# Embedding of images 2 to 7 as a two-tap filter with three products for two tokens

## The reference

```python
xp = jnp.pad(x, ((0, 0), (0, 0), (0, PAD), (0, 0)), mode='edge')   # 8 steps at the end
idx = jnp.arange(N)[:, None] * STRIDE + jnp.arange(PATCH_LEN)[None, :]   # patches of 16, stride 8: N = 16
patches = jnp.transpose(xp[:, :, idx, :], (0, 4, 2, 3, 1))
xf = jnp.fft.rfft(patches, axis=-2, norm='ortho')
x_emb = jnp.concatenate([real of xf, imag of xf], axis=-1) @ W.T   # 64 numbers per token
h = jnp.concatenate([cls_tok, x_emb], axis=1)      # 1 + 64*16 tokens per image
h = h + attention(layernorm(h))                    # causal, softmax, D = 64
h = h + experts(layernorm(h))                      # softmax gate over 8 experts, three layers each
```

## Time and profile before

| | us |
|---|---|
| median of 3 runs | 389.95 |
| the three runs | 384.7, 390.22, 389.95 |
| the profiled execution | 389.21 |
| its span, from the first to the last instruction | 387.5 |

### The profile page before, as it was taken

One profiled execution on the slowest core, in us unless ns is written; L12 is line 12 of the kernel. 1 busy time (PEld: TensorE's weight loads), 2 busy tenths in 40 slices (PEclk: granted clock), 3 DMA queues, 4 the chain that ended last, 5 costly groups with the idle time before them and its releaser, 6 DMA issues.

```text
span 387.5 us, 8012 instructions
## 1 busy us (share of the span) xinstructions
PE 366.3 (95%) x2670; PEld 167.1 (43%) x2670; DVE 267.4 (69%) x576; ACT 207.7 (54%) x435; POOL 125.4 (32%) x202
## 2 busy tenths in 40 slices
PE   4889899999999999999999999998999999999985
PEld 3555235444435435445435446345553333333321
DVE  3233656878878888887997999887345466656573
ACT  0234456556557647638638568567465456654510
POOL 6061211525435334344353454335314700000000
PEclk9999899999999999999999999996889999999999
DMA  6998920900900910820000000000000011100112
GB/s 154 223 176 180 216 42 4 216 1 2 210 10 2 188 28 0 166 51 0 0 1 3 2 0 2 1 3 0 3 0 3 2 27 29 29 10 18 30 28 56
DMA packets 28992, 20.45 MB, mean 53 GB/s; under 512 B 12280, under 2 KB 28832, under 8 KB 28960
## 3 DMA queue, kind: packets, MB, share of 16 engines
q1 hardware_dynamic: 28352, 19.91, 25.5%
q10 hardware_dynamic: 608, 0.12, 0.2%
HBM read 17.93 MB, written 2.10 MB: 52 GB/s over the span
## 4 chain that ended last, share of the span: by engine, by line
PE 76%; SPq 7%; ACT 5%; issue 4%; DVE 3%; DMA 3%; ACTq 0%; DVEq 0%
PE Sp L1231 13%; PE PTp L1246 8%; PE Sp L1442 7%; PE MM L1273 7%; PE MM L1185 6%; PE MM L1485 6%; PE PTp L1463 6%; PE MM L1188 5%; PE MM L1281 3%; DMA XW<-in_x_dram 3%; SPq L308 3%; PE MM L1211 2%; ACT EP L592 1%; PE PTp L1217 1%; ACT PT L532 1%
## 5 line engine op out<-in xcount | busy, mean ns | idle before, releaser
L1231 PE MATMUL Sp<-eT,G 64*64 64x512 f32 x512 | 74.4, 613 | 0.0
L422 POOL TENSOR_SCALAR_AFFINE_SELECT EP<-EP 128x128 f32<-128x128 f32 x64 | 23.5, 368 | 120.3 <-ACT EP L589 120.3
L532 ACT ACTIVATE PT<-PTp 128x512 f32<-128x512 f32 (+2 forms) x96 | 43.5, 489 | 28.4 <-PE PTp L1246 28.3
L834 DVE TENSOR_SCALAR_CACHE_REDUCE SN<-Sp,sr 128x1024 f32<-128x1024 f32 x32 | 41.0, 1281 | 10.2 <-PE Sp L1231 10.0
L834 DVE TENSOR_SCALAR_CACHE_REDUCE EP<-Sp,sr 128x1024 f32<-128x1024 f32 x32 | 40.8, 1280 | 9.9 <-PE Sp L1231 9.5
L843 DVE SCALAR_TENSOR_TENSOR SN<-SN,EP 128x384 f32<-128x384 f32 (+3 forms) x32 | 34.3, 1071 | 0.4 <-ACT EP L592 0.4
L1273 PE MATMUL MM<-PT,e 128*64 128x512 f32 (+3 forms) x176 | 31.4, 489 | 0.2
L1442 PE MATMUL Sp<-E2T,W1f 64*64 64x512 f32 x232 | 29.5, 615 | 0.2 <-ACT h L715 0.2
L1246 PEld LDWEIGHTS PTp<-ident,SN 128*128 128x128 f32 x176 | 19.5, 144 | 21.5 <-issue 18.0
L1083 DVE SCALAR_TENSOR_TENSOR PT<-PTp,negc,XW 128x512 f32<-128x512 f32 x28 | 19.7, 746 | 12.1 <-PE PTp L1463 11.5
L1231 PEld LDWEIGHTS Sp<-eT,G 64*64 64x64 f32 x512 | 15.3, 131 | 27.3 <-issue 27.1
(11 more groups left out here) (297 smaller groups left out, 671.1 us busy)
## 6 DMA issues: line engine op xcount, KB each, us to landing
XW<-in_x_dram SPq DMA_DIRECT2D x6, 1024.0 KB, 9.4
X<-in_x_dram SPq DMA_DIRECT2D x6, 1024.0 KB, 10.5
out_dram<-xc SPq DMA_DIRECT2D x8, 256.0 KB, 2.6
XW<-in_x_dram SPq DMA_DIRECT2D x2, 576.0 KB, 7.9
X<-in_x_dram SPq DMA_DIRECT2D x2, 576.0 KB, 13.6
XW<-in_x_dram SPq DMA_DIRECT2D x2, 448.0 KB, 11.4
X<-in_x_dram SPq DMA_DIRECT2D x2, 448.0 KB, 13.9
EP<-in_L_tok_W_dram SPq DMA_DIRECT2D x2, 144.0 KB, 3.0
```

The costliest lines, as they stand in the source:

```text
L422: pool.affine_select(out=blk_, in_=blk_, compare_op=ALU.is_ge, fill=0.0, base=0, pattern=[[-1, 128]], channel_multiplier=1).then_inc(tri_d ...
L532: return act.activation(dst, src, ACT.Copy)
L834: dve.tensor_scalar(W4[t % 4], Sp[t % 2][:, :], -SCALE, sr[q][:, place(t), 0:1], ALU.mult, ALU.min, accum_out=negm[q][:, t:t + 1]).then_in ...
L1231: ins = pe.matmul(Sp[t % 2][64 * s:64 * s + 64, CH * c:CH * c + CH], G[q][rows, 128 * t + 64 * s:128 * t + 64 * s + 64], eT[q][rows, :], **ON)
```

## The change

For images 2 to 7 the tokens are made in pairs. With blocks a = x_(2m+1), b = x_(2m+2):

- odd blocks: Z1 = W1 a (four products of 256 columns, into the first half of M0; raises yo_ready; ACT copies it to Z1 in SBUF at t = 2);
- even blocks: P = W0 x_(2m) (four products of 256 columns, into the second half of M0; raises ye_ready). The even token 2m is P + Z1, which DVE writes to Z at t = 4 (`z_even`);
- sums: XS = a + b, added by POOL in eight operations of 128x256 (`x_sum`, two at each of t = 0, 1, 2, and one at each of t = 3, 4; three and five at t = 3 and 4 in body 0), multiplied by W2E = 2E (four products of 256 columns, into the first half again). The odd token is 2E(a + b) - W1 a - W0 b, that is the product minus Z1 minus the next pair's P. DVE does it in two operations at t = 7, ahead of mask 7 (`z_odd`). The last one raises z_done, which `z_turn` waits for. XS lies in the tile h1, which is free until the experts.

`y_half(b, q, n)` with n = 0 to 11 takes the place of `y_piece`, and `load_x` has two more transfers of 16 KB for the edge block XP. DVE makes W2E and one edge weight once. The second copy of a body pair in the loops of POOL is written out for the last images, since they have no sums.

```diff
--- before.py
+++ after.py
@@ -104,11 +104,16 @@
         t2b = sb("t2b", [128, NPAIR, CH])
+        XS = h1[0].rearrange("p c a s -> p (c a s)")[:, 0:2048].rearrange("p (m r v) -> p m r v", m=8, r=4)
...
         Wef = sb("Wef", [128, 5, 2, D])
+        W2E = sb("W2E", [128, 4, D])
+        XP = [sb(f"XP{q}", [128, V]) for q in range(2)]
+        Z1 = sb("Z1", [128, CH // 2])
+        Z1v = Z1[:, :].rearrange("p (m v) -> p v m", m=8)
         A32 = sb("A32", [128, 2, D])
@@ -315,6 +322,9 @@
                                  src[:, :, half, :]).then_inc(ld_x[q], 16)
+                for half in range(2):
+                    edge = x[bass.ds(b, 1), :, T - 1, :].rearrange("a c v -> (a c) v")
+                    sp.dma_start(XP[q][64 * half:64 * half + 64, :], edge).then_inc(ld_x[q], 16)
@@ -360,6 +370,7 @@
             pool.memset(cst[:, 8:16], -0.5).then_inc(pool_steps, 1)
+            pool.memset(Wef[0:64, 4, 0, :], 0.0).then_inc(pool_steps, 1)
             pool.memset(agT[:, :], 0.0).then_inc(pool_steps, 1)
@@ -452,6 +463,15 @@
+            def x_sum(b, q, m):
+                if m == 0:
+                    pool.wait_ge(ld_x[q], at(32 * b + 32 - 32 * q))
+                    pool.sem_inc(passed_pool)
+                    pool.wait_ge(y_ready, at(b))
+                    pool.sem_inc(passed_pool)
+                other = X[q][:, 2 * m + 2, :, :] if m < 7 else bct(XP[q][:, :], 4)
+                pool.tensor_tensor(XS[:, m, :, :], X[q][:, 2 * m + 1, :, :], other, ALU.add).then_inc(xs_done, 1)
+
             pool.wait_ge(pool_steps, nth("const_set", 4))
@@ -460,13 +480,17 @@
-            def body(b, q, first=False, last=False):
+            def body(b, q, first=False, last=False, y_next=True):
                 late, end = 1 if first else 0, 1 if last else 0
...
                         tri(b + 1, 0)
+                    if y_next:
+                        for m in ((), (), (), (0, 1, 2), (3, 4, 5, 6, 7))[t] if first and t < 5 else () if first or t > 4 else \
+                                ((0, 1), (2, 3), (4, 5), (6,), (7,))[t]:
+                            x_sum(b + 2, q, m)
                     if not first:
@@ -495,10 +519,12 @@
             body(0, 0, first=True)
-            with pool.Fori(0, NB // 2 - 1) as j:
+            with pool.Fori(0, NB // 2 - 2) as j:
                 body(2 * j + 1, 1)
                 body(2 * j + 2, 0)
-            body(NB - 1, 1, last=True)
+            body(NB - 3, 1)
+            body(NB - 2, 0, y_next=False)
+            body(NB - 1, 1, last=True, y_next=False)
             last = Hb(NB - 1, QG, QG)
@@ -554,6 +580,11 @@
                 copy(Zv, M0[:, :].rearrange("p (n v) -> p v n", n=NTOK)).then_inc(z_done, 1)
+
+            def z1_copy(b):
+                act.wait_ge(yo_ready, at(b - 1))
+                act.wait_ge(z_done, at(b))
+                copy(Z1[:, :], M0[:, 0:256]).then_inc(z1_done, 1)
@@ -669,8 +700,8 @@
                         g_copy(b + 1, 1 - q)
-                    if t == 7 and y_next:
-                        z_copy(b + 2)
+                    if t == (3 if first else 2) and y_next:
+                        z1_copy(b + 2)
                     if t < NT - 1:
@@ -796,6 +827,9 @@
             dve.tensor_tensor(Wef[64:128, 4, 1, :], sumE[64:128, 4, :], sumO[64:128, 4, :], ALU.subtract).then_inc(dve_steps, 1)
+            dve.tensor_scalar(W2E[:, :, :], sumE[:, 0:4, :], 2.0, None, ALU.mult).then_inc(dve_steps, 1)
+            dve.scalar_tensor_tensor(out=Wef[64:128, 4, 0, :], in0=sumE[64:128, 4, :], scalar=-1.0, in1=sumO[64:128, 4, :],
+                                     op0=ALU.mult, op1=ALU.subtract).then_inc(dve_steps, 1)
             dve.wait_ge(act_steps, nth("c_sq", 1))
@@ -891,6 +925,19 @@
+            def z_even(b):
+                dve.wait_ge(ye_ready, at(b - 1))
+                dve.wait_ge(z1_done, at(b - 1))
+                dve.wait_ge(zt_ready, at(b))
+                dve.tensor_tensor(Zv[:, :, 0:NTOK:2], M0[:, 256:CH].rearrange("p (m v) -> p v m", m=8), Z1v, ALU.add).then_inc(zo_done, 1)
+
+            def z_odd(b):
+                dve.wait_ge(y_ready, at(b + 1))
+                dve.tensor_tensor(Zv[:, :, 1:NTOK:2], M0[:, 0:256].rearrange("p (m v) -> p v m", m=8), Z1v, ALU.subtract).then_inc(zo_done, 1)
+                dve.wait_ge(zo_done, at(2 * b - 2))
+                dve.tensor_tensor(Zv[:, :, 1:NTOK - 1:2], Zv[:, :, 1:NTOK - 1:2],
+                                  M0[:, 288:CH].rearrange("p (m v) -> p v m", m=7), ALU.subtract).then_inc(z_done, 1)
+
             ln1_centre(0)
@@ -936,7 +983,11 @@
                         class_arg(b, q, 1)
+                    if t == 7 and y_next:
+                        z_odd(b + 2)
                     mask(b, q, t)
+                    if t == 4 + late and y_next:
+                        z_even(b + 2)
                     if t == NT - 1 and not last:
@@ -1174,21 +1225,33 @@
-            def y_piece(b, q, n):
-
+            def y_half(b, q, n):
+
+                k, i = divmod(n, 4)
                 if n == 0:
-                    pe.wait_ge(ld_x[q], at(16 * b + 32 - 16 * q))
+                    pe.wait_ge(ld_x[q], at(32 * b + 32 - 32 * q))
                     pe.wait_ge(h_done, at(b))
+                if n == 4:
+                    pe.wait_ge(z1_done, at(b - 1))
+                if n == 8:
+                    pe.wait_ge(zo_done, at(2 * b - 3))
+                    pe.wait_ge(xs_done, at(8 * (b - 1)))
+                c0 = (0, 256, 0)[k]
+                weights = (Wef[:, i, 1, :], Wef[:, i, 0, :], W2E[:, i, :])[k]
                 for c in range(2):
                     vs = slice(32 * c, 32 * c + 32)
-                    if n < 4:
-                        pe.matmul(M0[64 * c:64 * c + 64, :], Wef[:, n, 0, :], X[q][:, :, n, vs],
-                                  start=(n == 0), stop=False, skip_group_check=True)
-                    else:
-                        pe.matmul(M0[64 * c:64 * c + 64, 0:CH - 32], Wef[:, n - 4, 1, :], X[q][:, 1:16, n - 4, vs],
-                                  start=False, stop=False, skip_group_check=True)
+                    blocks = (X[q][:, 1:16:2, i, vs], X[q][:, 0:16:2, i, vs], XS[:, :, i, vs])[k]
+                    ins = pe.matmul(M0[64 * c:64 * c + 64, c0:c0 + 256], weights, blocks,
+                                    start=(i == 0), stop=(i == 3 and k < 2), skip_group_check=True)
+                if n == 3:
+                    ins.then_inc(yo_ready, 1)
                 if n == 7:
-                    y_pad(q).then_inc(y_ready, 1)
+                    ins.then_inc(ye_ready, 1)
+                if n == 11:
+                    for c in range(2):
+                        ins = pe.matmul(M0[64 * c:64 * c + 64, 224:256], Wef[:, 4, 0, :], X[q][:, 15, 3, 32 * c:32 * c + 32],
+                                        start=False, stop=True, skip_group_check=True)
+                    ins.then_inc(y_ready, 1)
@@ -1375,7 +1438,8 @@
                     if t == 0 and y_next and not first:
-                        y_piece(b + 2, q, 0)
+                        y_half(b + 2, q, 0)
+                        y_half(b + 2, q, 1)
                     p_turn(b, t, late)
@@ -1385,8 +1449,9 @@
                     if y_next:
-                        for n in ((), (0, 1) if first else (1,), (2, 3), (4,), (5,), (6,), (7,), ())[t]:
-                            y_piece(b + 2, q, n)
+                        for n in ((), (), (0, 1, 2, 3), (4, 5, 6), (7,), (8, 9), (10, 11), ())[t] if first else \
+                                ((), (2, 3), (4, 5, 6), (7,), (), (8, 9), (10, 11), ())[t]:
+                            y_half(b + 2, q, n)
                         if t == 7:
```

## The result

The changed kernel takes 404.13 us (median; 402.35 to 408.31), the kernel before 390.09 on the same count; the ratio is 1.043 (95% interval 1.032 to 1.054). It is slower by 4%, 14 us. The forecast was 392 with 382 to 403 as its range. Executions of one kernel fall into fast and slow ones by the clock that was granted; the medians are of all of them, the ratios of the fast ones alone.

The account below looks back on a forecast made before the run. PE was taken to bound the kernel, with DVE only 4.5 us to spare per image. From 389.2 us: body 0 -1.2, five bodies at -1.55 + 1.3 + 0.6 make +1.8, clock +2.5: 392 us, 8 in 10 within 382 to 403.

Parts of the forecast that it names:

- PE's saving: Embedding products on PE at t = 2 to 4: 7.73 us become 6.18, 1.55 us less per image.
- The link at the body's end: Mask 7 on DVE waits behind z_odd, so PE waits ahead of tile 7's transposes: 1.3 us more per image.
- POOL's sums: Sums ahead of the root and add_rest delay DVE and PE's tile 4: 0 to 1.6 us per image, 0.6 taken.
- Interference: POOL's sums hold up DVE operations with two SBUF inputs: 0 to 0.73 us per sum, counted inside the 0.6.
- The clock: PE's clock falls at body ends: one and a half falls of 1.7 us over bodies 1 to 5, +2.5 us.
- Rival 1: The clock falls at nearly every body's end, six times 1.7 = 10 us more: 400 us; chance 0.22.
- Body 0: First body: PE no longer waits for image 2's transfer but for mask 2; gain 2.0 or 0.3 us, -1.2 taken.
- the case with a fall: Body 0 if the clock falls behind its wait as before: the gain is 0.3 us instead of 2.0.
- Rival 2: DVE becomes the bound at 32.5 us per image because POOL's sums block its two-SBUF-input operations: 403 us; chance 0.10.

Follow-up runs that it names:

- no_sums_z_behind: Changed kernel without POOL's eight additions (XS filled once with zeros) and with z_odd behind mask 7: 383.1 us, 0.991 of the kernel before; turn 28.79 us.
- dense_at_4: Changed kernel with halves 5 to 7 on PE moved to just ahead of tile 4's transposes: 399.3 us, 1.036 of the kernel before; turn 32.44 us.
- after_again: The changed kernel run once more with no edit: 401.7 us, 1.042 of the kernel before; turn 32.83 us.
- after: The changed kernel as first measured and profiled, against the kernel before: 404.13 us, ratio 1.043.
- z_odd_behind: Changed kernel with z_odd on DVE behind mask 7 in place of ahead of it: 398.0 us, 1.023 of the kernel before; turn 31.31 us.
- sums_write_only: Changed kernel with each POOL addition replaced by two fills of the same length together: 395.2 us, 1.024 of the kernel before; turn 31.38 us.

## Why the prediction was wrong

- **PE's saving, 1.55 us per image**: 1.27 in no_sums_z_behind. The direction and most of the size were right. The pieces gave back slightly more than was worked out (6.07 us for 6.18); what is missing went to the products with the values and with U, 0.37 longer, which the term had left as they were. Why these are longer was not tested. The wait for ACT's copy of U, 0.52 us, comes on top only with the sums.
- **The link at the body's end, 1.3 us**: 1.25 to 1.33 in bodies 0 to 5 of the changed kernel, and gone when z_odd moved. Right, though terms of it were off against each other: the first z_odd operation took 0.60, not 0.41, mask 7 began 0.30 behind the start of the second, and the hand-overs came to slightly less than 0.3.
- **POOL's sums, 0.6 us per image with 1.6 as the upper bound**: this is the step that failed. Measured 2.7 to 2.8 with all that follows: 1.1 to 1.2 by the queue, 1.1 to 1.2 by interference, and about 0.4 by the clock's falls behind the wait they caused. The way was right, sums, root, add_rest, DVE's second layer norm, smax 5, mask 4, PE at tile 4, each seen late in the trace by about what was worked out (add_rest 3.4 us against up to 2.9). But its own worked bound was 1.6 and even that, near which the wait at tile 4 lies (1.22), was then waved down to 0.6 because POOL "has the more idle time". Idle time in sum is no cover for an operation that stands in a particular wait: in the trace the four sums' 2.9 us came through nearly whole (1.5 at tile 3's triangle and 1.4 behind it), and contention added 0.5 on POOL itself. Over bodies 1 to 5 this term alone is 5 x 1.7 = 8.5 us too low without the falls, most of the 11 us between the forecast and the profiled execution (403.5 us).
- **Interference, "counted inside the 0.6"**: the failure's second half. The prediction looked at the large masks and at smax. What was hit in the changed kernel were four-column operations, of which there are many: one that takes 0.16 alone took up to 0.69, so it waited for most of a sum's 0.73. Two in a row at t = 1 alone cost 1.0 us (144.97 to 146.29). POOL's own operations were held up too, which the prediction left out.
- **The clock, 2.5 us over five bodies by falls at the body's end**: falls came (four in the first profile, three in the second), but at tile 4, behind the small products, and by dense_at_4 at 0.4 to 0.5 us a turn, 2 to 3 us in all. The size came out right by luck: two to three times as many falls as the one and a half forecast, each at 0.7 to 0.8 us and not 1.7, and at another place. Rival 1 (falls at nearly every body's end) didn't come.
- **Body 0, -1.2 us**: the wait moved to mask 2 as worked out (1.76 us for 1.7), the clock fell behind it as in the case with a fall, and the body gained 0.2 (0.3 had been worked out for that case). In after_again, the same kernel without a fall there, body 0 took 27.7, 1.8 less than before (2.0 worked out). Behind this same wait the clock fell in 6 of the 11 profiles that have it, so which case comes is not settled by the kernel.
- **Rival 2 (DVE becomes the bound), 403 us**: nearest in time, and its mechanism, the wait of DVE for POOL's reads, is part of the cause. But DVE was busy for 27.6 of 33 us and not full, so it wasn't the bound; the rest is order and waits. The rival put every sum at its whole 0.73 us, 5.8 in a turn, and the interference measured was 1.1 to 1.2.

What stays open: the total varies by up to 12 us between executions of one kernel, and this goes with the mean granted clock (381.6 us at 0.996, 393.3 at 0.969 for the kernel before). Why the clock falls at one place in one execution and at another in the next, as it did in the unchanged last stretch of all profiles, was not found and not controlled. In the two profiles compared first, the falls of the first and the last stretch nearly cancel (+3.6 and -4.5 us).

## What to carry to other kernels

Work that is moved to an engine with time to spare is priced by what stands behind it on that engine's queue, and by who waits for that; walk the queue step by step, and take the bound you get as the price unless a row shows the cover. Before adding many POOL operations beside a busy DVE, count the small DVE operations too, since each can wait for most of a POOL operation (0.5 of 0.73 us here). A result that another engine needs late goes behind, not ahead of, the wide operation that PE waits for: that one swap was worth 1.3 us per turn here.

## What was not expected of the hardware

- DVE operations of 4 columns took 0.65 to 0.69 us beside a POOL addition of 128x256 (0.15 to 0.20 in the kernel before), and at most 0.17 beside POOL fills of the same length: with those the turn was 1.6 us shorter, 1.1 of it without the clock's falls. It goes both ways: a POOL operation of 128x256 (pv) took 1.12 us beside DVE's mask 3, 0.61 in the kernel before.
- A DVE addition of two transposed 128x256 operands, one in PSUM and one in SBUF, took 0.60 us; one of 224 columns with only the PSUM operand transposed, into the same Z, took 0.39.
- Behind a wait of 1.1 to 1.3 us between small products and transposes the clock fell to 1.2 GHz in nine of fifteen bodies (after, after_again, z_odd_behind), behind a wait of 1.25 to 1.33 between score products and transposes in none of thirty. With three dense pieces ahead, a wait of 0.77 to 0.88 at tile 4 did not end in a fall either, nor did 0.66 without them (sums_write_only).
